# Second attention: the order in which TensorE's two row tiles take a step's products and scores

## What is computed

```python
def _L1_attn_ref(x, ln_g, ln_b, W_kv, W_x, W_xa, W_out):
    h = _layernorm(x, ln_g, ln_b)
    qk, v = jnp.split(h @ W_kv, 2, axis=-1)             # 16 heads of 8
    scores = jnp.einsum('bhqd,bhkd->bhqk', qk, qk)
    a1 = jax.nn.softmax(scores, axis=-1)
    a1 = jnp.einsum('gh,bhqk->bgqk', W_x, a1)           # heads mixed into heads
    o1 = jnp.einsum('bhij,bhjd->bhid', a1, v)
    return o1.transpose(0, 2, 1, 3).reshape(b, n, dims) @ W_out
```

## Time and profile before

| | |
|---|---|
| time, median of 3 runs | 1661.07 us (1660.34 to 1665.47) |
| the profiled execution | 1660.28 us, its span 1658.4 us |
| second attention, first to last product | 768.2 to 1513.3 us |
| PE busy, share of the span | 95% |
| DVE, ACT, POOL busy | 77%, 64%, 58% |

### The profile page before, as it was taken

One profiled execution on the slowest core, in us unless ns is written; L12 is line 12 of the kernel. 1 busy time (PEld: TensorE's weight loads), 2 busy tenths in 40 slices (PEclk: granted clock), 3 DMA queues, 4 the chain that ended last, 5 costly groups with the idle time before them and its releaser, 6 DMA issues. The chain is left out here.

```text
span 1658.4 us, 56350 instructions
## 1 busy us (share of the span) xinstructions
PE 1571.1 (95%) x17756; PEld 1120.3 (68%) x17756; DVE 1269.6 (77%) x3471; ACT 1062.7 (64%) x2468; POOL 967.8 (58%) x1129
## 2 busy tenths in 40 slices
PE   4999999999999889988999999999999999998998
PEld 3344444444444367765888888888888888887997
DVE  5778888888878479977777777777877777773666
ACT  0567777777777656763676666676676667774332
POOL 4445454544443045556877887778877788762222
PEclk7899999999999899997999999999999999999999
DMA  7333333333333100012222222222222222200111
GB/s 208 101 103 106 105 102 114 101 106 104 105 100 98 34 23 28 28 46 85 82 79 64 73 80 79 75 65 70 83 75 68 71 75 83 69 31 14 63 63 54
DMA packets 170167, 129.07 MB, mean 78 GB/s; under 512 B 13036, under 2 KB 143224, under 8 KB 170104
## 3 DMA queue, kind: packets, MB, share of 16 engines
q1 hardware_dynamic: 169136, 127.65, 24.9%
q10 hardware_dynamic: 968, 0.60, 0.1%
HBM read 60.56 MB, written 54.53 MB: 69 GB/s over the span
## 5 line engine op out<-in xcount | busy, mean ns | idle before, releaser
L817 DVE TENSOR_REDUCE shifts<-bank 128x2 bf16<-128x512 f32 x1024 | 693.2, 692 | 159.8 <-PE bank L972 146.0
L767 ACT ACTIVATE probs<-bank 128x512 f32<-128x512 f32 x1024 | 588.6, 594 | 156.6 <-PE bank L965 143.3
L911 PE MATMUL bank<-values,probs 64*128 64x129 f32 x8192 | 576.8, 279 | 0.7 <-DVE o_even L785 0.6
L911 PEld LDWEIGHTS bank<-values,probs 64*128 64x128 f32 x8192 | 508.7, 188 | 51.7 <-issue 26.8
L965 PE MATMUL bank<-q_stack,k_stack 49*128 49x256 bf16 x2048 | 384.8, 276 | 38.0 <-DMA q_stack<-shift_rows 27.9
L972 PE MATMUL bank<-k_stack,q_stack 48*128 48x256 bf16 x2048 | 388.7, 280 | 11.6 <-DMA q_stack<-score_parts 7.4
L593 POOL TENSOR_TENSOR values<-mix,v_in 128x1024 f32<-128x1024 f32 x128 | 301.3, 2364 | 3.0 <-ACT v_in L733 3.0
L965 PEld LDWEIGHTS bank<-q_stack,k_stack 49*128 49x128 bf16 x2048 | 145.2, 95 | 181.9 <-issue 76.7
L602 POOL TENSOR_TENSOR o_odd<-o_odd,scaled 128x256 f32<-128x256 f32 x224 | 162.9, 727 | 148.4 <-ACT scaled L697 148.4
L697 ACT ACTIVATE scaled<-bank,recips 128x128 f32<-128x128 f32 x448 | 139.2, 362 | 111.0 <-DVE recips L811 109.8
L902 PE MATMUL bank<-probs,values 128*32 128x256 f32 x2048 | 170.4, 406 | 0.0
(11 more groups left out here) (146 smaller groups left out, 2159.9 us busy)
## 6 DMA issues: line engine op xcount, KB each, us to landing
score_parts<-parts SPq DMA_DIRECT2D x128, 192.0 KB, 2.3
k_stack<-score_parts SPq DMA_DIRECT2D x256, 96.0 KB
q_stack<-score_parts SPq DMA_DIRECT2D x256, 96.0 KB
score_parts<-parts SPq DMA_DIRECT2D x128, 128.0 KB, 2.2
score_parts<-parts SPq DMA_DIRECT2D x128, 64.0 KB, 1.8
x_in_f<-x_all SPq DMA_DIRECT2D x64, 128.0 KB, 2.0
x_in<-in_L_attn_x SPq DMA_DIRECT2D x32, 128.0 KB, 3.1
q_stack<-shift_rows SPq DMA_DIRECT2D x256, 2.0 KB
```

What stands on the lines that cost most here:

```text
L767: act.activation(probs[:, s % RING, :, :].rearrange("p t n -> p (t n)"), s2[s % 2][:, :], ACT.Exp, scale=scale).then_inc(exp_done, 1)
L817: dve.tensor_reduce(shifts[:, :, hf, col], s1[s % 2][:, :].rearrange("p (t n) -> p t n", t=TILES), op=ALU.max, axis=AX.X, negate=True).the ...
L911: return pe.matmul(pv_bank(h)[:, q * (D + 1):(q + 1) * (D + 1)], probs[rows, h % RING, t, q * P:(q + 1) * P], values[b.odd][rows, t, h, :] ...
```

## The change

On PE, in the second attention, the products and the scores of a step are no longer two blocks that both row tiles go through together. The lower row tile does its four products and then its two scores; the upper one does its two scores and then its four products. The functions are cut into single matmuls (`lower_product`, `upper_product`, `second_score`, `first_score`), each with its own waits at its first matmul, and `rows_apart` sets their order. What is computed, the operands, the banks and all other engines' programs stay as they are. The first attention keeps its order (`both_scores`). The diff, cut to its core:

```diff
-        def products(i, on, s):
-            if lower:
-                lower_half_waits(*lower)
-            if upper:
-                pe.wait_ge(half_done, upper[0].number() * HEADS + (upper[1] + 1))
-            for q in range(TILES):
-                for t in range(TILES):
...
-                        product = half_of_products(*lower, 0, q, t)
...
-                        product = half_of_products(*upper, 1, q, t)
...
+        def upper_product(b, h, k):
+
+            if k == 0:
+                pe.wait_ge(half_done, b.number() * HEADS + (h + 1))
+            product = half_of_products(b, h, 1, k)
+            if k == TILES * TILES - 1:
+                product.then_inc(pv_done, 1)
...
+        def rows_apart(i, on, s):
...
+            def score(row_tile, t):
+                if s % 2 == row_tile:
+                    if on(0):
+                        second_score(i, s, t)
+                elif on(1):
+                    first_score(i.plus(1), s, t)
+
+
+            lower(0)
+            score(1, 0)
+            score(1, 1)
+            lower(1)
+            upper(0)
+            lower(2)
+            upper(1)
+            lower(3)
+            upper(2)
+            score(0, 0)
+            upper(3)
+            score(0, 1)
...
-                scores(i, on, s)
                 if first:
+                    both_scores(i, on, s)
...
-                    products(i, on, s)
+                    rows_apart(i, on, s)
```

More of the change, by code:

```diff
@@ L906, in products_by_group, with half_of_products @@
                 last.then_inc(pv_done, 1)
-        def half_of_products(b, h, half, q, t):
+        def half_of_products(b, h, half, k):
+            q, t = k // TILES, k % TILES
             rows = slice(half * TILE_ROWS, (half + 1) * TILE_ROWS)
             return pe.matmul(pv_bank(h)[:, q * (D + 1):(q + 1) * (D + 1)], probs[rows, h % RING, t, q * P:(q + 1) * P],
-                             values[b.odd][rows, t, h, :], start=(half == 0 and q == 0 and t == 0),
+                             values[b.odd][rows, t, h, :], start=(half == 0 and k == 0),
@@ L948, in scores, with lower_product @@
-        def scores(i, on, s):
-            if on(0):
-                if s % half_heads == 0:
[L951 to L955, removed]
+        def lower_product(b, h, k):
+            if k == 0:
+                if h == 0:
+                    pe.wait_ge(values_ready, (b.number() + 1) * (2 * TILES))
+                pe.wait_ge(exp_done, b.number() * HEADS + (h + 1))
+                if h == BESIDE:
+                    pe.wait_ge(shift_rows_ready, (b.number() + 1) * 2)
+                    pe.wait_ge(v_taken, times(b, 1, n))
+                else:
+                    count, odd = head_before(b, h)
+                    wait(pe, scaled_ready if odd else pv_taken, count * TILES)
+            product = half_of_products(b, h, 0, k)
+            if k == TILES * TILES - 1:
+                product.then_inc(half_done, 1)
@@ new lines, in upper_product, with second_score @@
+        def upper_product(b, h, k):
+            if k == 0:
+                pe.wait_ge(half_done, b.number() * HEADS + (h + 1))
+            product = half_of_products(b, h, 1, k)
+            if k == TILES * TILES - 1:
+                product.then_inc(pv_done, 1)
+        def second_score(b, s, t):
+            if t == 0:
+                if s % half_heads == 0:
+                    pe.wait_ge(shifted[s // half_heads], b.number() * 32 + 32)
+                wait(pe, exp_done, b.number() * HEADS + (s - 1))
+            rows = stack_rows(s % 2, HEAD_ROWS + 1)
+            score = pe.matmul(s2[s % 2][:, t * TOK:(t + 1) * TOK], core.k_stack[b.odd][rows, s // 2, t * P:(t + 1) * P],
+                              core.q_stack[b.odd][rows, s // 2, :], start=True, stop=True)
+            if t == TILES - 1:
+                score.then_inc(s_in_psum, 1)
```

48 lines of the change are left out of this document (17 added, 31 removed).

## The result

| | before | changed |
|---|---|---|
| time, median | 1660.7 us (1658.9 to 1665.5, 4 runs) | 1679.5 us (1674.7 to 1683.1, 4 runs) |
| ratio | | 1.0107, 95% interval 1.0073 to 1.0141 |
| the same again, later | 1664.7 us (28 runs) | 1674.3 us (11 runs), ratio 1.0057, 1.0032 to 1.0082 |
| first attention, first to last exponential | 524.8 us | 534.6 us |
| second attention, first to last exponential | 739.8 us | 751.3 us |

The changed kernel is slower, and the forecast was slower. The table also says that the 19 us of the first measurement are not all the change's. Of the profiled executions' 20, only 11.5 lie in the second attention. Ten lie in the first, whose length varies by itself (experiments 1, 2 and 4), and the later measurement gives 9.6. So the change costs 0.6 to 0.7%. The forecast had 22 us, all of them in the second attention.

What follows compares the result with a forecast made beforehand. The prediction took PE and the order on it to set the time. Its terms, -1.4 + 0.7 + 1.4 = +0.7 us a batch, over 32 batches made 22 us on 1660.3: 1682 us, range 1652 to 1708.

Steps and rivals of the forecast that it cites:

- The gap of the wait: Second attention, PE's wait for half_done: 0.155 us in nine of 16 steps goes away, -1.4 us a batch.
- The uncovered load: After seven full-array operations a batch, the lower tile begins with a product load that nothing covers: +0.7 us a batch.
- The new holds: PE's product loads wait for the chain from late first scores through DVE's maxima, reciprocals and sums: +1.4 us a batch.
- steps 12 to 14: Second attention, with norm statistics in DVE's chain: PE held 0.7 us in two waits, in steps 12 and 14.
- step 1: Second attention, only the maxima's transposes between: PE ready at S + 1.47, load allowed at S + 1.82, held 0.35 us.
- steps 2 to 7: Second attention, first scores wait for maxima: PE held 0.08 us in each of three pairs, 0.25 in all.
- steps 8 to 10: Second attention: carrying the durations through all sixteen steps added a tenth to the new holds here.
- S: Start of an odd step's last first score, from which the chain is timed in us; for steps 12 to 14, step 11's.
- The sum: All terms together: +0.7 us a batch, 22 us over 32 batches of the second attention, giving 1682 us.
- Rival A: Second attention: the new waits don't hold, only the first two terms stay, 1638 us, faster; chance 0.17.
- Rival B: Second attention: row tiles start matmuls in program order, eleven slots a step, +1.8 us a batch, 1718 us; chance 0.12.

Runs made afterwards that it cites:

- experiment 1: The changed kernel with the first attention's two waits back ahead of each step's first score, as before the change: 1673.3 us, 1.0055 of before.
- experiment 2: The kernel before, with the first attention's wait for the maxima moved behind the step's first score: 1663.0 us, 1.0013 of before.
- experiment 4: The changed kernel run again, unedited, against the kernel before: 1674.3 us, 1.0057 of before.
- experiment 3: The kernel before, with only the wait for half_done moved from ahead of all eight products to the first upper product: 1629.2 us, 0.979 of before.
- experiment 7: The changed kernel with the second attention's maxima over half the columns and the exponent scaled down (results no longer correct): 1653.8 us, 0.9953 of before.
- experiment 5: The changed kernel with DVE's maxima of odd steps 1 to 13 put behind the next even step's reciprocal and sums: 1676.1 us, 1.0102 of before.
- experiment 6: The changed kernel with DVE taking the odd head's reciprocal ahead of the even step's maxima: 1670.3 us, 1.0031 of before.
- experiment 8: The kernel before, with maxima over half the columns and the exponent scaled down, as a control: 1660.6 us, a batch 23.20 us.
- experiment 10: The kernel before with the half_done wait at the first upper product, and four lower products listed ahead of four upper ones: 1798.8 us, a batch 27.57 us.
- experiment 9: A repeat of the kernel before with only the half_done wait moved to the first upper product: 1626.3 us, 0.9793 of before.

## Why the prediction was right, and where only by chance

**The gap of the wait, −1.4: right in plain steps.** Plain pairs went from 2.55 to 2.25 and stay at ten slots a step, and experiment 3 shows the gap by itself. That experiment gets back 1.10 and not 1.40, though, because part of the gap stays ahead of a full-array operation. So how the −0.75 of this term and the next divides between them is a choice of accounting, and the new holds below are counted against it.

**The uncovered load, +0.7: right with the term above.** With 0.155 taken off for each removed gap, pair (8, 9) went from 3.02 to 3.11, (10, 11) from 2.58 to 2.69 and (14, 15) from 3.00 to 3.09: 0.09 to 0.11 for each return from a full-array operation, 0.65 for seven. Against experiment 3, which begins these steps with scores, the three pairs are only 0.03 to 0.06 longer. Not all of it need be the load: with shorter maxima (experiment 7) pairs (8, 9) and (10, 11) lose 0.04 and 0.05 again, which may be small holds.

**The new holds, +1.4: right in kind and in sign, partly right in place, too large.** They are 23.51 − (23.21 − 1.40 + 0.65) = 1.05 us a batch. This is the term that was mis-sized, and within it the line on steps 12 to 14:

| | predicted | measured |
|---|---|---|
| step 1 | 0.35 | 0.29 |
| steps 2 to 7 | 0.25 | 0.32, all of it in pair (6, 7) |
| steps 8 to 10 | 0.1 | none that could be told from the load's price |
| steps 12 to 14 | 0.7 | 0.40 |

(The measured column is in lengths of pairs. It has the load that nothing covers behind a hold, about 0.1, besides the hold itself.)

In steps 12 to 14 the prediction had two waits. There was one of any size, in step 14. The sums hold nothing in step 13 (experiments 5 and 7). In step 12 the load stood 0.27 behind the transposes' load (1050.52 to 1050.79), where an unheld one took 0.20 in experiment 7 (1068.87 to 1069.07), so at most 0.07 was lost there, to ACT's scaling, over at 1050.68. PE stood ready at S + 3.41 (1053.73, with S = 1050.32) instead of S + 3.26, and the load came at S + 3.68 instead of S + 3.95: a hold of 0.27, not 0.7. Two links were shorter than the rows from which they were taken. The statistics took 0.40 to the reciprocal (1051.23 to 1051.63), not 0.55. In the row of before an idle time of 0.08 stands ahead of the reciprocal (1014.73 + 0.47 to 1015.28), probably for PE's products; which wait ended it was not tried. And ACT's scaling followed the reciprocal after 0.18, not 0.29 (1053.09 to 1053.27). The prediction followed DVE alone here. It left out ACT's `x_t`, and with it the reason why no reordering of DVE's work frees this place.

In steps 2 to 7 the size, 0.25 against 0.32, was right by chance. The prediction let the maxima that PE's scores wait for hold PE 0.08 in each of three pairs. The pairs (2, 3) and (4, 5) run at 2.23 and 2.25, with no hold, and all of it is in pair (6, 7). For that one the prediction had named the cause, ACT's exponential behind the late scaling, without a price; a load in step 7 waits 0.16 for ACT's exponential and one in step 8 for the scaling (experiment 6).

**The sum.** 32 batches of +0.30 are 9.6 us, and the phase as a whole has 11.5, against 22. That 1682 stood so near to 1679.5 is partly luck: the first attention was longer by 10 us in the profiled execution of the changed kernel, and of the 22 us that the prediction put into the second attention only half are there.

**Rival A** (the holds don't hold) is refuted by the list of waits and by experiments 6 to 8, though its threshold was near: with 0.75 us of new holds instead of 1.05 the two kernels would be equal, and experiment 7, with 0.5 to 0.6 less, is faster than before. **Rival B** (row tiles in the program's order) is refuted for this program: plain steps take ten slots with bfloat16 scores on one tile beside float32 products on the other. But experiment 10 shows that it isn't wholly false. The row tiles run apart only over a short stretch of the list, and a list that asks for more pays 4.4 us a batch against before. The Trainium skill ("TensorE: Matmul & The Clock Gate", on the mechanism of row and column tiling) has matmuls start in program order. The pairs of 2.23 us, at ten slots a step, don't bear that out between two row tiles; experiment 10 shows how short the freedom is.

**The cause.** The change removes a gap of 0.155 us whose cause in plain steps was the place of a wait, and to that end moves scores to a step's end and products to its start, which takes from DVE the time in which it did the maxima of odd steps, and from ACT that in which it did the exponentials of even ones. DVE's part, 0.59 us a batch with maxima shorter by 0.27 each, is shown; that ACT's order sets what is left in step 14 is read from its rows in experiments 6 and 7, and no run changed it. Moving the wait alone (experiments 3 and 9) beats both kernels: 0.979 of before in both comparisons, where the changed kernel is 1.011 and 1.006 of it.

## What to carry to other kernels

If PE shows a gap at a wait whose matmul could run later than its neighbours, move the wait to that matmul before moving any matmul: a wait listed ahead of a group holds also those that don't need it. When an order on one engine moves, write down for its consumers the chain from the moved instruction through their fixed orders back to the buffer that the mover needs, and compare it with the time in which the mover returns; idle time of the consumers doesn't shorten this chain. Take the links of such a chain only from rows in which the operation waited for nothing but the one ahead of it. Write the chain for every consumer with an order of its own: here DVE's and ACT's ended within 0.05 us of each other, and shortening one gave almost nothing. And don't take idle time with a releaser's name for a hold until you have seen the same distance in a run in which that releaser was early.

## What the runs showed of the hardware

- Row tiles run apart, but only near each other in the list: four lower and four upper products in a row cost 4.4 to 5.5 us a batch over the same products in turn (27.57 against 23.21 and 22.11), and the second tile began 0.45 us behind the first (experiment 10, one run).
- PE goes on 0.05 us behind its releaser where the load itself has the wait (sums over at 1058.89, load at 1058.94), and 0.10 where the wait stands on an instruction ahead of the load (scaling over at 1053.90, load at 1054.00).
- DVE goes from its last operation of a pass through the loop to the first of the next in 0.67 us from start to start, where the same two operations inside a pass stand 0.34 (short maxima) or 0.61 (full ones) apart (experiment 7 and the changed kernel).
- The first attention took from 524.8 us (before) to 537.6 (experiment 3) in twelve profiles, and these two run the same program in it. The granted clock is not steady there as it is in the second attention. In the share table over that phase the granted clock is 0.96 for before (52 to 572 us) and 0.95 for experiment 3 (52 to 589 us), and one point of 525 us is 5 of the 13 us. What sets this length is left open; for a kernel like this one a phase's length says more than the total.
